# Delta-rule stage of an eight-stage network kernel: pieces in a list-scheduled order, shared PSUM banks, the 31-tap filter on ScalarE and GpSimd

## The chip, the cores and the metric

One core of one Trainium2 chip runs the whole program. The metric is device time in microseconds (us) of one execution. TensorE is called PE, VectorE DVE, ScalarE ACT, GpSimd POOL; DMAs of this stage are issued by the sync engine, SP.

## The reference

Eight stages work one after the other on a residual of 4 batches x 1024 tokens x 128 features in float32: attention, mixture of experts, Mamba block, mixture of experts, sparse attention, a ternary feed-forward block, the delta-rule block, and a ternary feed-forward block. The change lies in the seventh, whose core is this (H = 4 heads, DK = DV = CH = 32, L tokens):

```python
q = _l2norm(q); k = _l2norm(k)
v = v * beta[..., None]; kb = k * beta[..., None]
A = -jnp.einsum('bhncd,bhnsd->bhncs', kb, k) * jnp.tril(ones, -1)
for i in range(1, CH):
    A = A.at[..., i, :].add(jnp.einsum('bhns,bhnsc->bhnc', A[..., i, :], A))
inv = A + eye;  u = inv @ v;  w = inv @ kb
def step(S, xs):
    attn = (qi @ ki.T) * mt
    ui = ui0 - wi @ S
    oi = qi @ S + attn @ ui
    return S + ki.T @ ui, oi
```

Ahead of it q, k and v are projected, convolved causally over 4 tokens and passed through SiLU; beta is a sigmoid of a projection. Beside it v goes through four causal filters (FIR) of 3, 7, 15 and 31 taps for each channel. The four results, v itself and the delta rule's output are the six branches. A gate computes six weights for each head and token, from the hidden state and from each branch's mean absolute value: a GELU layer, a layer to logits, a softmax with a temperature and a floor of 0.05. The weighted sum of the branches is normalised for each head by its root mean square, projected and added to the residual.

## The kernel before, in words

`delta_stage` (L3060) holds features in partitions and tokens in columns: `xT` is 128 x 4096. A batch has 1024 tokens, that is 8 tiles of 128, 32 chunks of 32, 4 pairs of tiles, 2 halves of 512. The work is cut into named pieces, and `schedule()` yields one list of them. Each engine's program walks this one list and emits its own part of every piece, in the list's order. So each engine's queue is in order and fixed, and semaphores alone hold the queues together.

The list is made of: `preparation(b)`, with `raw` (projections of q, k, v), `beta`, `conv` (on DVE: L3595 and L3600), `silu` (ACT, with the squares), `unit` (a product with a block of ones sums the squares over the 32 rows of a head and leaves each sum in all of them, L3258; ACT takes the root, L3486; DVE inverts 128x1024, L3606) and `scale` (POOL L3227 and L3230, DVE L3611 and L3613); `pair_of_tiles(b, pair)`, with `cross` (transposes L3282 and products L3293), four rounds of `level` and `grow` that invert the triangular block (L3266), `uw`, and `keep` (L3341 to L3347), which makes each chunk's transition; and `finish(b)`, with 31 `step`s of the state (PE L3361, DVE L3669), 56 filter taps on DVE (`tap`, L3683 and L3686, one 128x1024 instruction each, one tap between two steps), and then for each half, one after the other: `ruled`, `stat` (ACT takes absolute values, L3524, PE averages them over heads, L3381), `hidden`, `logits`, `mix`, four `token` pieces (six transposes L3413, six products L3727, one reduction L3735), `square`, `root`, `o_scale`, `turn`, `out` (L3754).

What sets the order: `interleave` (L3047) runs the pairs of batch b two ways at a time and puts in, at fixed rates, the preparation of batch b+1 (`AHEAD_RATE` 0.5) and the finish of batch b-1 (`END_RATE` 1.9). The preparation of batch 0 stands alone at the beginning, behind the layer norm of all four batches (`norm.vector`, `norm.scalar`, `norm.tensor`, L275 transposes) and the tempering of the gates (L3569 to L3578), and the finish of batch 3 stands alone at the end.

PSUM has eight banks: the `cross` and `keep` pieces share four (0 to 3), `level`, `grow` and `uw` take turns on banks 4 and 5, and all other pieces take turns on banks 6 and 7 (`wide`, a ring of two). A piece's matmuls wait until the earlier user of their bank has been read.

## Time and profile before

| what | value |
|---|---|
| median of 3 runs | 4448.43 us (4441.52 to 4453.62) |
| the profiled execution, its own time | 4447.42 us |
| its span | 4445.6 us |
| the delta stage in it | 3208.0 to 4188.4 us |
| PE busy over the span | 3357.0 us (76%) |
| DVE busy | 3073.2 us (69%) |
| ACT busy | 2142.4 us (48%) |
| POOL busy | 841.6 us (19%) |
| granted PE clock, mean | 0.826 of full |

The profile is one execution, taken by the hardware profiler. Busy time of an engine is the time in which at least one of its instructions runs. The granted clock is the share of PE's full clock that the throttle let through, 1.0 being 2.4 GHz and 0.5 1.2 GHz. A group of instructions is given as: line, engine, operation, output<-inputs, shapes, count | busy us, mean ns of one | idle us of the engine just ahead of them, and what ended that. Timeline rows begin with the start and the length in us, and end in brackets with idle time ahead of them.

### The profile page before, as it was taken

The page shows a single profiled execution, that of the slowest core. Times are in us where ns is not written, and L with a number is a line of the kernel's source. Part 1 is how long each engine was busy: PE and PEld are TensorE (multiplying, and loading weights), DVE is VectorE, ACT ScalarE, POOL GpSimd, SP SyncE. Part 2 cuts the span into 40 slices and gives each one's busy share as a digit, 9 for nine tenths or more (in the row PEclk, how much of TensorE's full clock was granted, in tenths as well). Part 3 has the DMA queues.
Part 4 walks back from the last instruction along what each step waited for, and adds up shares of the span by engine and source line. Part 5 has one row for each costly group of instructions (what it writes and reads, how often), then busy time and mean ns, then how long its engine had stood idle before and what let it go on. Part 6 is the DMA issues. An engine that isn't in the chain of part 4 may idle for free. (4 is left out here: it accounts for less than half of the span.)

```text
span 4445.6 us, 85630 instructions
## 1 busy us (share of the span) xinstructions
PE 3357.0 (76%) x35482; PEld 1538.8 (35%) x35552; DVE 3073.2 (69%) x4612; ACT 2142.4 (48%) x3613; POOL 841.6 (19%) x734
## 2 busy tenths in 40 slices
PE   6999998996556566699788888879846474653699
PEld 1222222663112111256433333324424353542344
DVE  8889895876787787787634677744455858668543
ACT  4888887664533342266432666656431121110464
POOL 1000100552343344445431000010000000000100
PEclk7999999998667565699899999979966665665799
DMA  3100101000110101000143022010000000000000
GB/s 90 25 22 18 25 8 33 1 2 9 29 26 3 29 0 29 12 18 2 32 74 43 10 39 38 23 49 1 12 2 4 2 3 2 3 3 2 27 1 20
DMA packets 138474, 85.31 MB, mean 19 GB/s; under 512 B 94755, under 2 KB 109749, under 8 KB 137957
## 3 DMA queue, kind: packets, MB, share of 16 engines
q1 hardware_dynamic: 135336, 75.56, 8.0%
q0 software_dynamic: 2688, 4.20, 0.6%
q8 instruction: 283, 4.64, 0.4%
q14 instruction: 103, 0.84, 0.1%
q10 hardware_dynamic: 64, 0.07, 0.0%
HBM read 47.81 MB, written 18.60 MB: 15 GB/s over the span
## 5 line engine op out<-in xcount | busy, mean ns | idle before, releaser
L833 DVE TENSOR_REDUCE attn_peak_halves<-attn_ps 128x2 f32<-128x1024 f32 x512 | 601.6, 1219 | 58.3 <-PE attn_ps L664 50.6
L786 ACT ACTIVATE attn_weights<-attn_ps 128x512 f32<-128x512 f32 x1024 | 531.2, 601 | 100.9 <-PE attn_ps L692 100.8
L1342 PE MATMUL mamba_ps<-mamba_stack,mamba_spread 96*128 96x512 bf16 x512 | 205.1, 519 | 284.9 <-DVE mamba_driven L1566 141.6
L1508 POOL TENSOR_TENSOR mamba_out_c<-mamba_states,mamba_c_rep 128x1024 f32<-128x1024 f32 x128 | 321.8, 2514 | 487.9 <-DVE mamba_states L1572 476.1
L2690 DVE TENSOR_REDUCE sparse_peak<-sparse_ps 128x4 f32<-128x1024 f32 x256 | 309.4, 1224 | 134.1 <-PE sparse_ps L2320 132.6
L142 PE MATMUL moe_ps<-moe_xT_halves,moe_w_halves 128*128 128x512 f16 x1536 | 363.8, 384 | 10.1 <-DVE moe_w_halves L1106 5.9
L1089 POOL TENSOR_TENSOR moe_hidden<-moe_exact,moe_hidden 128x512 f16<-128x512 f32 x256 | 297.0, 1164 | 342.2 <-ACT moe_hidden L1073 333.7
L2550 ACT ACTIVATE sparse_weights<-sparse_ps 128x512 f32<-128x512 f32 (+1 forms) x512 | 272.1, 585 | 176.9 <-PE sparse_ps L2387 89.3
L692 PE MATMUL attn_ps<-attn_q_stack,attn_k_stack 50*128 50x512 f16 x1024 | 321.4, 386 | 30.5 <-ACT attn_weights L786 7.1
L142 PE MATMUL ffn_ps<-ffn_layers,ffn_h_halves 128*128 128x512 f16 x1536 | 334.4, 379 | 3.6 <-ACT ffn_gate L2919 3.6
L1572 DVE TENSOR_TENSOR_SCAN mamba_states<-mamba_ps,mamba_driven 128x1024 f32<-128x1024 f32 x128 | 293.2, 2291 | 33.0 <-ACT mamba_ps L1484 17.3
L1484 ACT ACTIVATE mamba_ps<-mamba_ps,mamba_rates 128x1024 f32<-128x1024 f32 x128 | 138.3, 1086 | 296.5 <-PE mamba_ps L1342 295.9
L664 PE MATMUL attn_ps<-attn_k_stack,attn_q_stack 48*128 48x512 f16 x1024 | 270.7, 395 | 13.9 <-DVE attn_peak_halves L833 12.6
L2991 DVE TENSOR_TENSOR ffn_layers<-ffn_exact,ffn_layers 128x512 f16<-128x512 f32 x192 | 133.1, 695 | 208.1 <-ACT ffn_layers L2908 207.5
L3686 DVE SCALAR_TENSOR_TENSOR delta_branch<-delta_v,delta_fir_w,delta_branch 128x1024 f32<-128x1024 f32 x208 | 271.9, 1307 | 2.5
L704 PE MATMUL attn_ps<-attn_weights,attn_values 128*9 128x512 f32 x2048 | 269.4, 598 | 0.0
L1152 DVE SCALAR_TENSOR_TENSOR moe_exact<-moe_ps,moe_gate 128x512 f32<-128x512 f32 x256 | 175.1, 686 | 84.9 <-ACT moe_gate L1065 79.4
L1566 DVE TENSOR_TENSOR mamba_driven<-mamba_ps,mamba_b_rep 128x1024 f32<-128x1024 f32 x128 | 155.0, 1211 | 94.4 <-PE mamba_ps L1342 94.4
L1065 ACT ACTIVATE moe_gate<-moe_ps 128x512 f32<-128x512 f32 x256 | 152.0, 594 | 137.9 <-PE moe_ps L142 134.0
L142 PEld LDWEIGHTS ffn_ps<-ffn_layers,ffn_h_halves 128*128 128x128 f16 x1536 | 150.0, 98 | 184.3 <-issue 4.5
L692 PEld LDWEIGHTS attn_ps<-attn_q_stack,attn_k_stack 50*128 50x128 f16 x1024 | 80.4, 94 | 374.7 <-ACT attn_weights L786 283.0
L142 PE MATMUL moe_ps<-moe_w_halves,moe_hidden 128*128 128x128 f16 x3072 | 193.6, 220 | 18.3 <-POOL moe_hidden L1089 13.7
(463 smaller groups left out, 6130.1 us busy)
## 6 DMA issues: line engine op xcount, KB each, us to landing
mamba_stack<-mamba_parts SPq DMA_DIRECT2D x96, 128.0 KB, 2.4
sparse_factor<-sp_factor SPq DMA_DIRECT2D x24, 256.0 KB, 3.6
sp_halves<-sparse_parts SPq DMA_DIRECT2D x8, 512.0 KB, 3.0
ffn_h<-in_h SPq DMA_DIRECT2D x4, 1024.0 KB, 7.8
attn_q_stack<-attn_halves SPq DMA_DIRECT2D x96, 32.0 KB
attn_k_stack<-attn_halves SPq DMA_DIRECT2D x96, 32.0 KB
attn_halves<-attn_hp SPq DMA_DIRECT2D x8, 384.0 KB, 3.3
attn_q_stack<-attn_peak_rows SPq DMA_DIRECT2D x128, 2.0 KB
```

What stands on the lines that cost most here:

```text
L142: made = pe.matmul(out, a, b, start=first and i == 0, stop=last and i == 2)
L664: made = pe.matmul(use.slot[:, p, :], q_stack[rows, slot, couple, t * P:(t + 1) * P], k_stack[rows, slot, couple, half_of(keys)], start=Tr ...
L692: pe.matmul(use.slot, k_stack[rows, slot, couple, k * P:(k + 1) * P], q_stack[rows, slot, couple, half_of(half)], start=True, stop=True).t ...
L704: made = pe.matmul(out_acc[32 * h:32 * h + HD + 1, :], values[:, b % 2, k, first + h, :], weights[:, step_no(g, half, k) % 2, h, :], start ...
L786: act.activation(weights[:, at % 2, h, :], use.slot, ACT.Exp).then_inc(*key_act.one())
L833: dve.tensor_reduce(peak_halves[:, turn % PEAKS, keys, at:at + 2], use.slot, AX_X, ALU.max).then_inc(*score_dve.one())
L1089: pool.tensor_tensor(low, exact_sb[:, i % 3, :], hidden[:, i // EB % 3, i % EB, 0, :], ALU.subtract).then_inc(*hidden_low.one())
L1508: pool.tensor_tensor(out_c[:, n % 6, :], states[:, n % 3, :], c_rep[:, b % 2, :], ALU.mult).then_inc(*product_made.one())
L1572: dve.tensor_tensor_scan(states[:, n % 3, :], use.slot, driven[:, n % 2, :], 0.0, ALU.mult, ALU.add).then_inc(*steps_dve.one())
L2550: act.activation(weights[:, at % 2, h, begin:], use.slot[:, begin:], ACT.Exp).then_inc(*key_act.one())
L2690: dve.tensor_reduce(peak[:, at % PEAKS, unit // 2, 4 * r:4 * r + 4], use.slot.rearrange("p h (a k) -> p (h a) k", a=2), AX_X, ALU.max).the ...
L3686: dve.scalar_tensor_tensor(branch[:, n, :], shifted_v, weight, branch[:, n, :], ALU.mult, ALU.add).then_inc(*tapped.one())
```

## The change

One function, `delta_chains()`, names all pieces as chains with their dependences, and a list scheduler, `in_order()`, puts them into one order. It takes assumed costs (`PIECE_COST`), a hop of 0.08 us between engines, and 6 banks; at each turn it takes the piece that could begin first, less 0.02 of its distance to the end. Both ends change with it: the norm's parts are pieces of their own, batch by batch (`moments`, `norm_root`, `apply`, `features`), and the tempering comes after the first `scale`; `ruled`, `stat` and `token` are chains of their own, the statistics one piece for each branch, with `ruled` needing only the steps of its half.

PSUM: banks 0, 1, 2, 3, 6, 7 are shared; `cross` and `keep` still take 0 to 3 together, `level` and `grow` of one way keep one bank (4 or 5), `uw` takes shared banks, the statistics hold bank 6 or 7 from their first piece to their last.

Lengths: the squares are summed with tokens in partitions (`sums`), root and inverse are taken on 128x64, and `spread` multiplies with the identity to bring each inverse back to the 32 rows of its head, from where ACT copies it to `lengths`.

The 31-tap filter is a chain `long_tap`: for each tap and half ACT writes v times its weight into `weighted`, and POOL adds it onto the branch, which lies in `q_all`. ACT writes a half again only when POOL has added the tap before. DVE keeps 25 taps a batch.

The token sum has two products of 128x384 in place of six of 128x128, and three additions in place of the reduction. The weights' loads are reordered, with a semaphore of their own for the first four.

```diff
+LONG = len(FIR_TAPS) - 1
-TAP_ORDER = [(k, n) for k in range(max(FIR_TAPS)) for n, count in enumerate(FIR_TAPS) if k < count]
+TAP_ORDER = [(k, n) for k in range(max(FIR_TAPS)) for n, count in enumerate(FIR_TAPS) if n != LONG and k < count]
+STAT_ORDER = [4, 0, 1, 2, 3, 5]
+PIECE_COST = {
...
+    "level": [("pe", 0.8), ("dve", 0.45)], "grow": [("pe", 1.05), ("dve", 0.9)],
+    "uw": [("pe", 1.2), ("act", 0.8)], "keep": [("pe", 2.5), ("dve", 0.85), ("act", 0.45)],
+    "step": [("pe", 0.35), ("dve", 0.22)], "tap": [("dve", 1.25)], "long_tap": [("act", 1.35), ("pool", 2.6)],
...
+HOP, URGENCY = 0.08, 0.02
+SHARED = [0, 1, 2, 3, 6, 7]
...
+def delta_chains():
...
+        if b:
+            needs["raw", b, 0] += [("scale", b - 1)]
...
+        if b >= 2:
+            needs["beta", b] += keeps(b - 2)
+        if b >= 3:
+            needs["conv", b, 1] += [("token", b - 3, 1, TPC - 1)]
...
+        needs["ruled", b, half] += [("step", b, CPB // 2 - 2 if half == 0 else CPB - 2)]
...
+        needs["stat", b, half, 1] += [("tap", b, len(TAP_ORDER) - 1)]
+        needs["stat", b, half, 4] += [("long_tap", b, FIR_TAPS[LONG] - 1)]
+        needs["stat", b, half, 5] += [("ruled", b, half)]
...
+def in_order():
...
+            begin, _ = run(piece, ready, Counter(free), filled)
+            score = begin - URGENCY * to_end[piece]
+            if best is None or score < best[0]:
+                best = (score, which, piece, ready, filled)
...
@@ gpsimd
+                def long_tap(b, k):
+                    for half in range(HALVES if k else 0):
+                        so_far = long_of(b)[:, columns(half)]
+                        pool.wait_ge(*long_scaled.at(HALVES * (b * FIR_TAPS[LONG] + k) + half + 1))
+                        if k > 1:
+                            pool.wait_ge(*long_added.at(added_by(b, k - 1, half)))
+                        pool.tensor_tensor(so_far, so_far, weighted[:, half, :], ALU.add).then_inc(*long_added.one())
@@ tensor
-                norm.tensor(pe)
-                pe.wait_ge(*loads.at(16 * len(given)))
-                pe.wait_ge(*begun.at(1))
-                pe.wait_ge(*gained.at(1))
-                pe.wait_ge(*norm.featured.at(CHUNKS))
...
+                def sum_squares(b):
...
+                    for n in (1, 0):
+                        for t in range(TPB):
+                            at = (n * TPB + t) * KH
+                            made = pe.matmul(use.slot[:, at:at + KH], lengths[:, n, t * P:(t + 1) * P], first_of_head,
+                                             start=True, stop=True)
...
+                def spread_over_heads(b, n):
...
+                        for t in range(TPC):
+                            for h in range(KH):
+                                of_head = roots[:, 1, n, half * TPC + t, h:h + 1].broadcast_to([P, KD])
+                                made = pe.matmul(use.slot[KD * h:KD * (h + 1), t * P:(t + 1) * P], of_head,
+                                                 net.ident[:], start=True, stop=True)
...
@@ scalar
+                def long_tap(b, k):
...
+                    for half in range(HALVES):
+                        if k > 1:
+                            act.wait_ge(*long_added.at(added_by(b, k - 1, half)))
...
+                        act.activation(weighted[:, half, :] if k else long_of(b)[:, columns(half)],
+                                       v_all[:, b % 3, at:at + BANK], ACT.Copy,
+                                       scale=fir_w[:, tap:tap + 1]).then_inc(*long_scaled.one())
@@ vector
-                def invert_lengths(b, n):
-                    dve.wait_ge(*wide_act.at(one("unit", b, n).over))
-                    dve.reciprocal(lengths[:, n, :], lengths[:, n, :]).then_inc(*unit.one())
+                def invert_lengths(b):
+                    dve.wait_ge(*wide_act.at(one("sums", b).over))
+                    dve.reciprocal(roots[:, 1].rearrange("p n t h -> p (n t h)"),
+                                   roots[:, 0].rearrange("p n t h -> p (n t h)")).then_inc(*unit.one())
...
+                        dve.tensor_tensor(by_head(product[:, some, :]),
+                                          by_head(use.slot[:, 0:3 * P].rearrange("p (n d) -> p n d", n=3)),
+                                          weight.broadcast_to([P, 3, KH, KD]), ALU.mult).then_inc(*wide_dve.one())
...
+                    settle(dve.tensor_tensor(product[:, 0:3, :], product[:, 0:3, :], product[:, 3:6, :], ALU.add))
+                    settle(dve.tensor_tensor(product[:, 0, :], product[:, 0, :], product[:, 1, :], ALU.add))
...
-                    dve.tensor_reduce(o[:, t, :], product[:].rearrange("p n d -> p d n"), AX_X,
-                                      ALU.add).then_inc(*combined.one())
+                    dve.tensor_tensor(o[:, t, :], product[:, 0, :], product[:, 2, :], ALU.add).then_inc(*combined.one())
```

## Rows read from the trace of the kernel before

**Rows 1.** Busy time over stretches of the delta stage; its opening, middle, taps, end, whole
```profile
core 0: us, PE busy (x) PEld busy (x) DVE busy (x) ACT busy (x) POOL busy (x), PEclk, DMA share, GB/s
3208.00:3287.50 79.50, 25.02 (x58) 11.84 (x59) 49.60 (x126) 26.37 (x39) 4.30 (x2) 0.61 0.06 16
3287.50:4038.00 750.50, 443.74 (x15472) 325.26 (x15470) 504.28 (x843) 154.70 (x299) 16.64 (x6) 0.65 0.01 3
4038.00:4111.20 73.20, 12.17 (x376) 7.91 (x376) 71.04 (x88) 0.59 (x1) 0.00 (x0) 0.50 0.00 1
4111.20:4188.40 77.20, 47.65 (x288) 29.84 (x288) 31.73 (x84) 22.79 (x32) 0.00 (x0) 0.65 0.00 1
3208.00:4188.40 980.40, 528.59 (x16192) 374.85 (x16192) 656.65 (x1139) 204.45 (x371) 20.94 (x8) 0.63 0.01 4
```

**Rows 2.** Groups of DVE instructions of the stage, shapes kept apart
```profile
L3686 DVE SCALAR_TENSOR_TENSOR delta_branch<-delta_v,delta_fir_w,delta_branch 128x1024 f32<-128x1024 f32 x208 | 271.9, 1307 | 2.5
...
L3606 DVE RECIPROCAL delta_raw<-delta_raw 128x1024 f32<-128x1024 f32 x8 | 52.1, 6537 | 19.2 <-ACT delta_raw L3486 19.2
...
L3735 DVE TENSOR_REDUCE delta_o<-delta_product 128x128 f32<-128x768 f32 x32 | 46.8, 1461 | 1.1
...
L3727 DVE TENSOR_TENSOR delta_product<-delta_ps,delta_logits 128x128 f32<-128x128 f32 x192 | 40.8, 282 | 0.7
...
L3634 DVE TENSOR_TENSOR delta_t<-delta_ps,delta_masks 128x256 f32<-128x256 f32 x64 | 26.8, 421 | 62.6 <-PE delta_ps L3266 62.1
...
L3754 DVE TENSOR_TENSOR residual<-residual,delta_ps 128x512 f32<-128x512 f32 x8 | 5.5, 688 | 21.5 <-PE delta_ps L3430 21.5
```

**Rows 3.** The stage's waits, one row
```profile
ACT delta_absolute L3524 <- DVE delta_branch L3692: 174.3, 8, 73.1
```

**Rows 4.** Timelines of POOL and DVE around the scaling, batches 0 and 2
```profile
3280.50 2.00 POOL L3227 TENSOR_TENSOR delta_qk<-delta_qk,delta_raw 128x1024 f32<-128x1024 f32 x1 [275.57 <-DVE delta_raw L3606]
...
3282.53 3.34 DVE L3611 TENSOR_TENSOR delta_kbq<-delta_qk,delta_beta 128x1024 f32<-128x1024 f32 x1 [2.11 <-POOL delta_qk L3227]
...
3502.91 2.88 POOL L3227 TENSOR_TENSOR delta_qk<-delta_qk,delta_raw 128x1024 f32<-128x1024 f32 x1 [153.39 <-DVE delta_raw L3606]
...
3504.51 5.65 DVE L3686 SCALAR_TENSOR_TENSOR delta_branch<-delta_v,delta_fir_w,delta_branch 128x1024 f32<-128x1024 f32 x2
```

**Rows 5.** Earlier stages: a POOL product (MoE), a DVE product by min/median/max (Mamba)
```profile
L1089 POOL TENSOR_TENSOR moe_hidden<-moe_exact,moe_hidden 128x512 f16<-128x512 f32 x256 | 297.0, 1164 | 342.2 <-ACT moe_hidden L1073 333.7
...
L1551 DVE TENSOR_TENSOR mamba_temp<-mamba_temp,mamba_x x8: 1225/3250/3251, 1129.5 to 1699.1; 128x1024 f32<-128x1024 f32 x8
```

**Rows 6.** Groups of ACT instructions of the delta stage
```profile
L3524 ACT ACTIVATE delta_absolute<-delta_branch 128x512 f32<-128x512 f32 x40 | 24.4, 628 | 190.8 <-DVE delta_branch L3692 174.3 <-PE delta_ps L3381 16.5
...
L3534 ACT ACT_TABLE_LOAD x8 | 10.3, 1283 | 0.1
```

**Rows 7.** PE groups of the stage; the last row gives durations min/median/max
```profile
L3258 PE MATMUL delta_ps<-delta_raw,delta_block_ones 128*128 128x512 f32 x32 | 22.0, 825 | 22.3 <-ACT delta_raw L3480 22.3
...
L3402 PE MATMUL delta_ps<-delta_w_logit,delta_hidden 128*128 128x24 f32 x128 | 22.5, 297 | 6.2 <-ACT delta_hidden L3534 6.2
...
L3266 PE MATMUL delta_ps<-delta_n,delta_at 32*32 32x32 f32 x4096 | 63.7, 223 | 35.6 <-issue 13.2 <-DVE delta_n L3629 12.5 <-DVE delta_n L3644 9.7
...
L3244 PE MATMUL delta_ps<-delta_xT,delta_w_qkv x48: 592/1061/1222, 3233.0 to 3655.7; 128*128 128x512 f32 x48
```

**Rows 8.** Timeline of PE in the stage's opening
```profile
3214.46 2.14 PE L275 MATMUL delta_ps<-w_ident,delta_branch 128*128 128x128 f32 x8 [7.20 <-DVE delta_branch L215]
...
3233.02 7.17 PE L3244 MATMUL delta_ps<-delta_xT,delta_w_qkv 128*128 128x512 f32 x9 [4.87 <-DVE delta_eps L3578]
...
3262.98 5.68 PE L3258 MATMUL delta_ps<-delta_raw,delta_block_ones 128*128 128x512 f32 x8 [19.62 <-ACT delta_raw L3480]
```

**Rows 9.** Timeline of DVE: two steps of the state in the last batch
```profile
4040.25 0.18 DVE L3669 TENSOR_TENSOR delta_state<-delta_ps,delta_keep 128x32 f32<-128x32 f32 x1
...
4041.01 0.18 DVE L3669 TENSOR_TENSOR delta_state<-delta_ps,delta_keep 128x32 f32<-128x32 f32 x1
```

**Rows 10.** Timeline of PE: the statistics of a half in the last batch
```profile
4112.71 7.44 PE L3381 MATMUL delta_ps<-delta_absolute,delta_stat_select 128*128 128x512 f32 x12 [33.67 <-ACT delta_absolute L3524]
```

More of the change, by code:

```diff
@@ L1 @@
-from collections import Counter
+from collections import Counter, defaultdict
 from contextlib import ExitStack
@@ new lines, with __init__, take @@
+class Banks:
+    def __init__(self):
+        self.n, self.over, self.before = Counter(), Counter(), {}
+    def take(self, kind, by, slot, *filled):
+        self.n[kind] += 1
+        self.over[kind, by] += 1
+        earlier = {self.before[bank] for bank in filled if bank in self.before}
+        newest = {key: max(count for other, count in earlier if other == key) for key, _ in earlier}
+        for bank in filled:
+            self.before[bank] = ((kind, by), self.over[kind, by])
+        return Use(slot, self.n[kind], sorted(newest.items()), self.over[kind, by])
@@ L3154, in finish @@
-        def finish(b):
-            taps = [("tap", b, i) for i in range(len(TAP_ORDER))]
-            work = [[("step", b, c), taps[c]] for c in range(CPB - 1)] + [[tap] for tap in taps[CPB - 1:]]
-            for half in range(HALVES):
-                work += [[(what, b, half)] for what in ("ruled", "stat", "hidden", "logits", "mix")]
-                work += [[("token", b, half, t)] for t in range(TPC)]
-                work += [[(what, b, half)] for what in ("square", "root", "o_scale", "turn", "out")]
-            return work
@@ L3186, in delta_stage @@
-        uses, crosses, turns = {}, {}, {}
-        for piece in schedule():
-            if piece[0] in takes:
-                ring, by, count = takes[piece[0]]
-                uses[piece] = [ring.take(by) for _ in range(count)]
+        order, taken = in_order()
+        psum, uses, crosses, turns, kept = Banks(), {}, {}, {}, {}
+        by_act = ("features", "raw", "beta", "sums", "spread", "heads", "uw", "hidden", "turn")
+        all_heads = lambda width: ps[:, 0:CPT, 0:width * KC].rearrange("p a (m t n) -> p a m t n", m=2, t=2)
@@ new lines, in delta_stage @@
+        for piece in order:
+            if piece[0] in BANKS_OF:
+                by = "act" if piece[0] in by_act else "dve"
+                uses[piece] = [psum.take("wide", by, ps[:, bank, :], bank) for bank in taken[piece]]
+            if piece[0] == "stat" and piece[3] == 0:
+                uses[piece] = [psum.take("stat", "act", ps[:, bank, :], bank) for bank in taken[piece]]
+            if piece[0] in ("level", "grow"):
+                bank = 4 + piece[2] % 2
+                uses[piece] = [psum.take("diag", "dve", ps[:, bank, 0:8 * KC], bank)]
@@ L3196, in delta_stage @@
         pair_no = lambda b, pair: b * PAIRS + pair
+        last_keep = lambda b: max((("keep", b, pair) for pair in range(PAIRS)), key=lambda piece: kept[piece])
         grid_of = lambda slot: slot.rearrange("p (h t n) -> p h t n", h=KH, t=2)
@@ L3220, in _ @@
+                for piece in order:
+                    if piece[0] == "long_tap":
+                        long_tap(*piece[1:])
                     if piece[0] == "scale":
                         b = piece[1]
-                        qk, kbq = qk_all[:, b % 2], kbq_all[:, b % 2]
-                        pool.wait_ge(*unit.at(2 * b + 2))
+                        q, k, kbq = q_all[:, b % 3, :], k_all[:, b % 2, :], kbq_all[:, b % 2]
+                        pool.wait_ge(*wide_act.at(one("spread", b, 0).over))
```

542 lines of the change are left out of this document (333 added, 209 removed).

## The prediction, made blind

> **What bounds the kernel now.** I read first the busy times over the stretches of the delta stage [rows 1]. The stage takes 980.4 us (3208.0 to 4188.4), and no other stage is touched. In it the vector engine (DVE) is busy 656.7 us, TensorE (PE) 528.6, ScalarE (ACT) 204.5, GpSimd (POOL) 20.9: no engine fills the stage, and what counts is how badly they overlap. The stretches tell three different stories. The opening of 79.5 us is one chain through the first batch. The middle of 750.5 us has PE at 59% and DVE at 67%. The last 150.4 us are nearly serial: 73.2 us in which DVE alone works (71.0 busy, PE 12.2), then 77.2 us of gating, token sums and output projection for two halves, one after the other. Second, the groups of DVE work [rows 2]: the filter taps (L3686) are 271.9 us, 41% of DVE; the two full-width reciprocals a batch (L3606) 52.1; the weighted sum over branches (L3727, L3735) 87.6. Third, one line of the waits [rows 3]: ACT stands 174.3 us ahead of the absolute values, 73.1 of them once, because the queue puts the whole block of taps ahead of `ruled`. So the stage is bound by the written order at both ends and by DVE, in bursts, between them.
>
> **Against which time.** The profiled execution took 4447.4 us by its own time, 4445.6 of it span, 1.0 us under the median of 4448.4. I work against 4447.4; the 1.0 us is below what matters. Some 0.3% (13 us) is what a measurement of this kernel can tell from no change.
>
> **DVE.** (a) The 31-tap branch leaves it: 30 instructions a batch of L3686's form, 120 x 1.307 = 156.8 us, and four opening multiplies that cost no more than such a tap each, 160 in all [rows 2]. (b) Eight reciprocals of 1024 columns (52.1) become four of 64 columns; scaled by columns one is 0.4 us, so 50 goes. (c) A group of 128 tokens now costs (40.8 + 46.8)/32 = 2.74 us. After: two products of 384 columns, between the 421 ns of 256 columns and the 688 of 512 [rows 2], so 0.55 each; one addition of 384 columns, 0.55; two of 128, 0.28 each: 2.2 us. Over 32 groups 17 us goes. DVE is left with 656.7 - 160 - 50 - 17 = 430 us.
>
> **POOL.** It gains 30 additions x 2 halves x 4 batches = 240 of 128x512. Bounds: half of the 2.00 us that an undisturbed addition-sized operation of 1024 columns takes [rows 4], 1.00 us, and the 1164 ns of the MoE stage's 512-column product [rows 5]. I take 1.10: 264 us, with the 17 that stays (undisturbed) 281.
> DVE and POOL don't run such work side by side. At 3282.53 a DVE product that is 1.2 us by itself took 3.34: it waited for POOL's to end. From 3502.91 the two take turns: POOL's 2.00 becomes 2.88 behind one tap, and two taps take 5.65 us around POOL's operations [rows 4]. In the Mamba stage the same product takes 1.225 us or 3.251 [rows 5]. So every overlap of a two-SBUF-input operation is paid by one side. Of DVE's remainder such work is 88 taps and 36 convolution taps of the same form at 1.2 [rows 2] and some 70 us of small ones, about 220 us; in a middle of 600 us it stands in POOL's way a third of the time. 240 x 1/3 x 0.6 us is about 50 us for POOL, and DVE, by the same count the other way, loses about 65 us. At none this is 0 (the operations never meet), at most 264 us (DVE waits out every addition).
> The Trainium skill (SBUF — State Buffer, Who interferes with whom) says that the pair of ports is an exclusive lock for the whole instruction, and that a reduction never contends while a two-input addition does. The trace agrees on the lock; by the second clause the 96 new additions of the token sum are exposed where the 32 reductions were not, which would give back up to half of the 17 us of (c).
> The Trainium skill (GPSIMD Engine Reference, 3.1 Elementwise) keeps elementwise work on DVE, since GpSimd takes 1.96 times as long, 4497 ns for 2048 columns. An estimate by that page is 1.12 us an addition, 270 us in all; the rule would bite only if POOL's chain were the longest, which is the rival B below.
>
> **ACT.** 248 scaled copies of 128x512 from SBUF, at the 628 ns of the absolute values [rows 6]: 156 us. Roots over 64 columns in place of 16 of 512 save 8, plain copies of the spread lengths give them back. Interleaving may split runs of one table: 10 loads more at 1283 ns [rows 6] would be 13. ACT comes to 360 to 375 us of about 730: not a bound by itself, but its queue is in order, and a long tap waits there for POOL's addition one tap before.
>
> **PE.** Out: the block-ones product, 22.0 us [rows 7]. In: per batch 32 small instructions for the sums, at 0.15 us like the logits' twelve in about 1.0 us or up to 0.3 (their mean each), so 5 to 10, I take 6; and 128 instructions that spread an inverse over 32 rows. If four head rows overlap as the 32x32 blocks do (4096 instructions in 63.7 us busy [rows 7]) these are 5 to 6 us a batch; if not at all, at 0.2 us, 26. I take 6, because the trace's narrow tiles do overlap: 48 us in for 22 out. PE is left with 528.6 + 26 = 555 us, with an end of 635. It is now the busiest engine, and the cover for every other edit.
>
> **The opening.** Before, the first projection starts at 3233.0 after all four batches' norms and the gates' tempering; the first batch's transposes start at 3214.5 and take 2.1 us [rows 8]. Only they are wanted: with 0.6 us of eviction [rows 6] the projection starts at about 3217.5, 15.5 earlier. Then 30 us unchanged to the squares. From there to POOL's scaling it was 17.5 us [rows 4, 8]; now 6 (sums) + 1.6 (table, root) + 0.5 + 6 (spread) + 1.2 = 15.3. The opening goes from 79.5 to about 62 us (bounds 58 to 90). The loads' reordering costs nothing: four early weights are issued by about 3210, long before they are read; the norms of batches 1 to 3 slip under convolution waits.
>
> **The end.** After the last `keep` of batch 3: 15 steps at no more than 0.76 us, the beat that they keep with a short tap between them [rows 9], 11; `ruled` 2.6; of the 77.2/2 = 38.6 us a half takes, the 7.4 us of six statistics [rows 10] are done beforehand save the last (1.2), so 32 [rows 1]; of the second half, whose statistics and gates run under the first's tokens, some 20 remain. That is 66, taken as 70, against 150.4 plus the few us of keeps before it. The long taps of batch 3 must be ready: at 2 x (1.10 + 0.2) + 0.1 = 2.7 us a tap they take 84 us a batch and start at its scaling, some 150 us before the last keep, so about 60 us are to spare.
>
> **The middle.** PE has 555 - 25 (opening) - 45 (end) = 485 us to do; DVE 430 - 35 - 30 = 365 and 65 of waiting, 430; POOL some 270 + 50. Steps, taps and both ways of a batch are separate chains, and six banks replace a ring of two, so PE is rarely without work; but order is fixed from assumed costs and every queue waits in it, and the four banks of a cross or keep must all be empty. The middle of before had PE at 59%. I take 81%: 596 us.
>
> **Sum.** 62 + 596 + 70 = 728 us for 980.4: 252 less, 4447.4 - 252 = 4195 us.
>
> **Rivals.** *B, the shared ports decide.* POOL is slowed by taps, ACT stands at the long taps behind it, and PE's evictions behind ACT. For it: [rows 4, 5]. Against: most of DVE's small work reads PSUM, and 60 us are to spare. Price at full exclusion: 430 + 281 in series + 240 handovers x 0.1, with 65 us at the ends where neither works: 800; 4267 us.
> *C, PE packs better and its clock rises.* The granted clock was 0.65 over the middle at 59% busy and 0.50, the lower of the two levels (1.2 of 2.4 GHz), where PE was nearly idle [rows 1]; a wide projection takes 592 ns at best and 1222 at worst [rows 7]. With a denser queue some 300 us of wide instructions would fall by a quarter. 555 - 75 = 480, 410 of it in the middle, at 80% 510 us: stage 640, 4107 us. The Trainium skill (TensorE: Matmul & The Clock Gate, Part 1) says that activity releases the throttle, which speaks for C.
> *D, slower than before.* The long taps run in lockstep: ACT copies a half, POOL waits for a DVE tap, adds, and only then ACT goes on. A half then costs ACT 0.63 + 1.2 + 1.1 = 2.93 us: 248 x 2.93 = 727, plus ACT's other 180, 62 at the start and 55 at the end: 1024, 4491 us. It decides from 2.75 us a half. Against: there are two half buffers, and the copy of one goes under the addition of the other.
> *E, the order doesn't do what it says.* Real durations differ, the fixed queues drift, and the middle stays near 70% PE: 690 us, stage 822, 4289 us. I count it with B.
>
> **How the numbers follow.** My case 0.53, B and E 0.23, C 0.20, D 0.04. The range 4100 to 4300 holds my case with its bounds (opening to 90, PE to 635 at 81%: +110; no port waits: -40), C, B and E; beyond it lie D and some 0.1 of the tails of C and E. Faster by over 0.3%: all but D and a little of E, 0.95; within 0.3% 0.01; slower 0.04.
>
> **What would show it.** Right: the stage near 730 us; L3686's form down to 88 instructions; POOL with 240 additions of 1.0 to 2.3 us, mean near 1.3; taps on DVE partly stretched to 2.3 us; the first projection near 3217; no stretch with DVE alone at the end; PE above 75% of the middle. Wrong: ACT idle ahead of the scaled copies for over 100 us, waiting for POOL (B, D); PE under 70% with waits on `keep`, or on evictions (E); the clock above 0.8 (C); spreading above 15 us a batch.

## The result, and the profile after

The changed kernel takes 4396.66 us (median of four runs, 4390.06 to 4402.06), the kernel before on the same chip 4445.43: a ratio of 0.9887 with a 95% interval of 0.9864 to 0.991. That is 49 us less where 252 were forecast. The profiled execution is the one of 4390.06 us. In it the delta stage, from the first batch statistics on the vector engine to the last addition to the residual, goes from 979.7 to 924.1 us. Below, "stage" is always this stretch of a kernel's own profile.

Busy time over the stretches that answer to [rows 1]: the opening up to the first cross product, the middle up to the last `keep`, the end, and the whole.
```profile
core 0: us, PE busy (x) PEld busy (x) DVE busy (x) ACT busy (x) POOL busy (x), PEclk, DMA share, GB/s
3206.00:3261.00 55.00, 28.12 (x198) 19.55 (x198) 27.96 (x87) 22.38 (x32) 4.31 (x2) 0.69 0.09 24
3261.00:4038.30 777.30, 456.39 (x15928) 344.25 (x15928) 487.64 (x746) 314.57 (x556) 375.21 (x246) 0.65 0.01 3
4038.30:4130.40 92.10, 55.67 (x674) 34.76 (x674) 49.70 (x115) 24.69 (x35) 0.00 (x0) 0.70 0.00 1
...
3206.00:4130.40 924.40, 540.18 (x16800) 398.56 (x16800) 565.30 (x946) 361.64 (x622) 379.52 (x248) 0.66 0.02 4
```
Both ends are shorter than before: 55 us for 79.5 (62 were forecast), and 92 for 150.4 (70 were forecast). The middle is not: it is longer than before (777.3 against 750.5), and TensorE is still at 59% of it (456.4 / 777.3), the share it had before. Here the forecast said 596 us at 81%. Of the 196 us of stage that are missing (924.4 against 728), the middle has 181 and the end 22, and the opening gives 7 back.

The groups of instructions of the stage, shapes kept apart, for what the change added or touched [rows 2, 6]:
```profile
L3359 POOL TENSOR_TENSOR delta_q<-delta_q,delta_weighted 128x512 f32<-128x512 f32 x240 | 361.1, 1534 | 357.5 <-ACT delta_weighted L3734 357.5
L3734 ACT ACTIVATE delta_weighted<-delta_v,delta_fir_w 128x512 f32<-128x512 f32 x240 | 166.8, 722 | 82.7 <-POOL delta_q L3359 82.5
L3898 DVE SCALAR_TENSOR_TENSOR delta_branch<-delta_v,delta_fir_w,delta_branch 128x1024 f32<-128x1024 f32 x88 | 146.7, 1667 | 0.8
...
L3950 DVE TENSOR_TENSOR delta_product<-delta_product 128x384 f32<-128x384 f32 x32 | 26.6, 831 | 1.1
L3951 DVE TENSOR_TENSOR delta_product<-delta_product 128x128 f32<-128x128 f32 x32 | 26.5, 828 | 1.1
...
L3413 PE MATMUL delta_ps<-delta_block_ones,delta_raw 128*128 128x4 f32 x128 | 23.6, 321 | 2.6 <-ACT delta_raw L3660 2.6
...
L3424 PE MATMUL delta_ps<-w_ident,delta_roots 128*32 128x128 f32 x512 | 20.9, 331 | 0.4 <-issue 0.3
L3955 DVE TENSOR_TENSOR delta_o<-delta_product 128x128 f32<-128x128 f32 x32 | 20.8, 648 | 1.1
L3808 DVE SCALAR_TENSOR_TENSOR delta_v<-delta_raw,delta_conv_w,delta_v 128x1024 f32<-128x1024 f32 x12 | 20.3, 1695 | 0.0
```
The 88 taps are there, but each takes 1667 ns where it took 1307; the two additions of 128 columns take 828 and 648 ns where 0.28 us was forecast, and the sums and the spreading on TensorE take 44.5 us in all, where 48 were forecast.

The waits of TensorE in the stage (what it waited for: us in total, times, longest):
```profile
PE delta_ps L3534 <- DVE delta_state L3878: 107.5, 81, 9.8
PE delta_ps L3433 <- issue: 58.8, 40, 2.2
PE delta_ps L3466 <- DVE delta_kat L3833: 31.9, 5, 8.8
PE delta_ps L3433 <- DVE delta_n L3838: 28.8, 10, 7.1
PE delta_ps L3556 <- ACT delta_absolute L3710: 23.2, 19, 3.6
PE delta_ps L275 <- DVE delta_branch L196: 22.9, 2, 16.0
```
Two rows stand out. Ahead of the steps of the state TensorE waits 107.5 us for DVE. And 58.8 us, 40 times, it "waits" in the small blocks of the level products (L3433) for nothing that the profile shows. Before, this row had less than half of that:
```profile
PE delta_ps L3266 <- issue: 22.1, 19, 2.1
```
The timeline of TensorE in one such stretch (start, length, what it ran, in brackets the idle time ahead of it):
```profile
3303.57 1.20 PE L3433 MATMUL delta_ps<-delta_n,delta_at 32*32 32x32 f32 x69 [1.29 <-issue]
3304.54 1.04 PE L3433 MATMUL delta_ps<-delta_t,delta_n 32*32 32x32 f32 x58
3307.30 1.21 PE L3433 MATMUL delta_ps<-delta_t,delta_n 32*32 32x32 f32 x70 [1.72 <-issue]
3308.63 1.00 PE L3433 MATMUL delta_ps<-delta_n,delta_at 32*32 32x32 f32 x57
3311.03 1.20 PE L3433 MATMUL delta_ps<-delta_n,delta_at 32*32 32x32 f32 x71 [1.40 <-issue]
```
From halt to halt there are 69 + 58 = 127 and 70 + 57 = 127 matmuls, each with a weight load, and 3.7 us. The halts fall in the midst of a piece, where the code waits for nothing. Of the 40, 39 last 0.8 to 2.2 us and one 0.3. The DMA table of the stage has a queue that fits this count:
```profile
q8 instruction: 133, 2.18, 1.0%
```
133 packets and 2.18 MB are 16.4 KB a packet, and 33,600 matmuls and weight loads over 133 packets are 253 a packet: about one packet for each 127 matmuls with their loads.

The trace has the time of each packet too, and it says more than the count. Over all lines of the stage, 69 pauses of TensorE are put down to "issue" (96.5 us in all). Of these, 67 end 1.2 to 1.6 us after the queue's last packet before them is through; of the 174 other pauses of TensorE 7 do. From one such pause to the next there are 127 matmuls or a multiple of it, to within two, 59 times in 68. So these pauses are waits for the packets of this queue, and what the packets bring is TensorE's instructions. Where TensorE works less densely most packets come without a pause: there are 133 packets and 69 pauses.

So there were three suspects for the missing 196 us of stage: the shared access of DVE and GpSimd, the order itself with its round trips between TensorE and DVE, and the supply of TensorE's instructions.

### The profile page after: what moved, and what is told of

Same layout as the page of the kernel before. It is cut to its first block and busy times, and to the rows that moved or that the text cites. A ratio compares the mean times of both kernels' runs of the same rounds, so it can differ in the third digit from the quotient of the medians.

```text
span 4388.3 us, 87460 instructions
## 1 busy us (share of the span) xinstructions
PE 3362.3 (77%) x36090; PEld 1558.9 (36%) x36160; DVE 2982.4 (68%) x4420; ACT 2298.6 (52%) x3864; POOL 1198.0 (27%) x974
## 5 line engine op out<-in xcount | busy, mean ns | idle before, releaser
L3359 POOL TENSOR_TENSOR delta_q<-delta_q,delta_weighted 128x512 f32<-128x512 f32 x240 | 361.1, 1534 | 357.5 <-ACT delta_weighted L3734 357.5
L3734 ACT ACTIVATE delta_weighted<-delta_v,delta_fir_w 128x512 f32<-128x512 f32 x240 | 166.8, 722 | 82.7 <-POOL delta_q L3359 82.5
```

Of the source, the lines that this page charges most:

```text
L3359: pool.tensor_tensor(so_far, so_far, weighted[:, half, :], ALU.add).then_inc(*long_added.one())
```

## Experiments, first batch: what the long filter costs

All start from the changed kernel unless another is named. The kernel before took 4461.18 us on this chip. Chips differ by more than some of these edits do, so the stages are compared with each other. Most experiments are single executions, and the batches ran on different chips. The one kernel that was profiled twice, on two chips, gave stages of 766.3 and 770.4 us, so a difference of some 5 us or less is not to be read.

**GpSimd's additions on 8 columns** (the long filter's sum is left out but for these columns).
```
-  pool.tensor_tensor(so_far, so_far, weighted[:, half, :], ALU.add)
+  pool.tensor_tensor(so_far[:, 0:8], so_far[:, 0:8], weighted[:, half, 0:8], ALU.add)
```


> POOL's 240 additions of the long filter work on 8 columns in place of 512, so most of the 31-tap sum is left out; order, waits and ACT's copies stay. The delta stage of the changed kernel takes 924 us. Ports theory (what DVE and POOL take from each other, some 120 us of stretched DVE work, ate the gain): the stage falls by 120 us or more, to 800 or less. Order theory (PE and DVE wait for each other in one fixed order, the stretching is only part): it falls by 30 to 70, to 855 to 895. ACT theory (ACT's queue stands at the long taps): it falls by over 80 as well, and the next run by more.

Measured: 4311.26 us, stage 846.2, 78 less. Groups of its DVE instructions:
```profile
L3898 DVE SCALAR_TENSOR_TENSOR delta_branch<-delta_v,delta_fir_w,delta_branch 128x1024 f32<-128x1024 f32 x88 | 112.9, 1283 | 0.9
...
L3950 DVE TENSOR_TENSOR delta_product<-delta_product 128x384 f32<-128x384 f32 x32 | 17.9, 558 | 1.1
L3808 DVE SCALAR_TENSOR_TENSOR delta_v<-delta_raw,delta_conv_w,delta_v 128x1024 f32<-128x1024 f32 x12 | 15.3, 1278 | 0.0
...
L3955 DVE TENSOR_TENSOR delta_o<-delta_product 128x128 f32<-128x128 f32 x32 | 9.4, 293 | 1.1
L3951 DVE TENSOR_TENSOR delta_product<-delta_product 128x128 f32<-128x128 f32 x32 | 9.3, 292 | 1.1
```
The same instructions fall from 1667 to 1283 ns (taps), from 1695 to 1278 (convolution), and from 831, 828 and 648 to 558, 292 and 293 (token additions). The timelines of the changed kernel show one such meeting: while GpSimd adds without a break, a token addition of 128x128 takes 1.24 us, about as long as one of GpSimd's own, and 0.29 right after GpSimd's last.
```profile
3512.26 16.14 POOL L3359 TENSOR_TENSOR delta_q<-delta_q,delta_weighted 128x512 f32<-128x512 f32 x12 [2.71 <-ACT delta_weighted L3734]
```
```profile
3513.98 1.24 DVE L3951 TENSOR_TENSOR delta_product<-delta_product 128x128 f32<-128x128 f32 x1
...
3528.85 0.29 DVE L3951 TENSOR_TENSOR delta_product<-delta_product 128x128 f32<-128x128 f32 x1
```
DVE's busy time goes from 565.3 to 446.7: GpSimd costs DVE 119 us, of which 34 are in the taps, 17 in the convolutions and 37 in the token additions. The stage falls by 78. That is the price of GpSimd's additions as a whole and not of the shared access alone: the edit also takes 277 us of work off GpSimd (379.5 to 102.4) and shortens ScalarE's waits for it (82.5 to 4.9). But the stage is still 846 us with no long filter to speak of, so the larger part of what was missing lies elsewhere.

**ScalarE's copies on 8 columns too.**
```
-  act.activation(weighted[:, half, :] if k else long_of(b)[:, columns(half)],
-                 v_all[:, b % 3, at:at + BANK], ACT.Copy,
+  wide = 8 if k else BANK
+  act.activation((weighted[:, half, :] if k else long_of(b)[:, columns(half)])[:, 0:wide],
+                 v_all[:, b % 3, at:at + wide], ACT.Copy,
```


> ACT's 240 scaled copies are on 8 columns too, so the long filter costs neither ACT nor POOL anything; same order. Ports and order theory: within 15 us of the run with narrow additions alone. ACT theory: at least 40 us below it.

Measured: 4293.54 us, stage 831.9, 14 less than with narrow additions, while ACT falls from 351.8 to 255.6 us. ACT's 96 us were nearly all hidden.

**The long taps back on DVE**, the order planned with 1.25 us for each; all else of the change stays.
```
-    "step": [("pe", 0.35), ("dve", 0.22)], "tap": [("dve", 1.25)], "long_tap": [("act", 1.35), ("pool", 2.6)],
+    "step": [("pe", 0.35), ("dve", 0.22)], "tap": [("dve", 1.25)], "long_tap": [("dve", 1.25)],
...
+                def long_tap(b, k):
...
+                        dve.scalar_tensor_tensor(long_of(b), shifted_v, weight, long_of(b), ALU.mult, ALU.add).then_inc(*long_added.one())
```


> The long taps go back to DVE as their own chain of 31 full-width taps, and the same scheduler orders all pieces with 1.25 us for each; banks, ends, lengths and token sum stay as changed. By the loads alone (my prediction's way) DVE gets 160 us more and the stage gets longer by 60 us or more, to over 985. Ports theory: 120 us of stretching go, 160 of work come: 940 to 980. Order theory: the engines have room and no lock, 860 to 925: moving the filter was worth nothing.

Measured: 4414.65 us, stage 945.4. So the move of the filter brought 21 us, and everything else (order, banks, ends, lengths, token sum) 34 (979.7 to 945.4).

**The token's three additions as one reduction again.**
```
-  settle(dve.tensor_tensor(product[:, 0:3, :], product[:, 0:3, :], product[:, 3:6, :], ALU.add))
-  settle(dve.tensor_tensor(product[:, 0, :], product[:, 0, :], product[:, 1, :], ALU.add))
...
-  dve.tensor_tensor(o[:, t, :], product[:, 0, :], product[:, 2, :], ALU.add).then_inc(*combined.one())
+  dve.tensor_reduce(o[:, t, :], product[:].rearrange("p n d -> p d n"), AX_X, ALU.add).then_inc(*combined.one())
```


> The three additions of a token sum are one reduction over six again; all else as changed. Additions took 831, 828 and 648 ns where they were forecast at 550, 280 and 280. Ports theory: 73.9 us of additions become 46.8 of reductions that never wait, and POOL gets through sooner: the stage falls by 20 to 40. Order theory: by 0 to 15.

Measured: 4386.63 us, stage 919.0, DVE 538.0 us for 565.3.
```profile
L3953 DVE TENSOR_REDUCE delta_o<-delta_product 128x128 f32<-128x768 f32 x32 | 47.8, 1494 | 1.1
```
The reduction is the cheaper one here: the additions add to 831 + 828 + 648 = 2307 ns beside GpSimd's work, against 558 + 292 + 293 = 1143 beside its narrow additions, and the reduction takes 1494, hardly more than before (1461). DVE's 27 us give 5 at the end, which is within what two executions differ by: an engine that has time to spare.

## Second batch: order, round trips, instruction supply

**Another order of the same pieces.** The planner's table starts from the durations that the profile shows, scaled kind by kind (`keep` is 5.17 for 4.5 measured, `temper` 13.55 for 5.0), and an offset for each kind is added to its score. The values were found by a search off the chip; what they are worth is what the chip shows. Only the order differs, and with it the shared bank that a piece takes; the instructions and what they compute are the same.
```
-    "uw": [("pe", 1.2), ("act", 0.8)], "keep": [("pe", 2.5), ("dve", 0.85), ("act", 0.45)],
...
+    "uw": [("pe", 2.01), ("act", 1.17)], "keep": [("pe", 5.17), ("dve", 0.92), ("act", 0.69)],
...
+LATER = {"o_scale": -0.95, "cross": -1.16, "root": -14.5, "ruled": 0.85, "mix": -1.14, "moments": 0.8, "conv": 0.64, "norm_root": -24.59,
...
-HOP, URGENCY = 0.08, 0.02
+HOP, URGENCY = 0.05, 0.0145
...
-            score = begin - URGENCY * to_end[piece]
+            score = begin - URGENCY * to_end[piece] + LATER.get(piece[0], 0.0)
```


> Same instructions as the changed kernel; only the order of the pieces is another, planned from the durations that the trace of the changed kernel shows (keep on TensorE 4.5 us where the planner had 2.5, first convolution 5.2 for 4.2, token 3.3 for 1.95, and so on), with an offset for each kind of piece. The stage is 924 us long in the changed kernel. If the order is what holds the stage (waits between engines that another order could fill): 20 to 90 us less, stage 835 to 905, with TensorE's busy time unchanged near 540 and its share of the stage up from 58% to 60 to 65%. If the shared access of VectorE and GpSimd sets the stage whatever the order: within 15 us of 924, and the busy time of both unchanged (565 and 380). If the order on record is already near what the round trips allow: the same or slower.

Measured: 4276.49 us against 4442.77 for the kernel before, stage 809.9: 114 us less, more than the highest figure expected. The same 100 us by the clock (one of the stretches in which the two differ most), first with the order on record, then with the new one, and below that the new one's whole stage:
```profile
3406.00:3506.00 100.00, 52.06 (x1265) 33.55 (x1269) 73.23 (x90) 42.17 (x68) 55.16 (x30) 0.63 0.01 2
```
```profile
3406.00:3506.00 100.00, 70.76 (x2008) 49.74 (x2007) 72.35 (x114) 48.73 (x81) 47.18 (x32) 0.69 0.01 3
3206.50:4016.40 809.90, 530.68 (x16800) 397.75 (x16800) 549.76 (x943) 362.24 (x621) 384.05 (x248) 0.67 0.02 4
```
The order on record leaves stretches in which TensorE has little to do beside the steps: 1265 matmuls here, 52% busy. In the new order the small blocks of the next batch lie between them: 2008 matmuls, 71%. Over the stage the engines are as busy as before to within 16 us each. Of the 114 us, 105 are idle time of TensorE, which goes from 924.1 - 540.2 = 384 to 279 us.

**Long taps on DVE with an order of their own**: the kernel with all taps on DVE, and an edit of the same kind of its table, offsets and two constants, with values that were searched for this arrangement.


> The third experiment (long filter back on VectorE, GpSimd with nothing but the scales; stage 945 us) with its order planned from the durations measured there. If the move of the filter matters little and the order much: stage 840 to 900, so faster than the changed kernel at 924 without any help from GpSimd. If VectorE's load (594 us) is what holds this arrangement: 930 to 950, no gain from a better order. TensorE's busy time stays near 545 and VectorE's near 590 either way.

Measured: 4238.57 us, stage 766.3, well under the 840 to 900 expected. The order is worth 179 us to this arrangement (945.4 to 766.3), and it now beats the one with GpSimd and ScalarE by 44 (766.3 against 809.9). TensorE is at 68% (521.8), DVE at 77% (591.2). Each has its own order, so the 44 us compare the best found of each, not the filter's place alone.

**No recurrence between chunks** (left out: each step's product reads the batch's first state, and TensorE does not wait for the previous step).
```
-                    else:
-                        pe.wait_ge(*wide_dve.at(one("step", b, c - 1).over))
...
-                                         state[rows, b % 2, c, :], start=True, stop=True)
+                                         state[rows, b % 2, 0, :], start=True, stop=True)
```


> Left out: the recurrence from one chunk's state to the next; each step's product reads the batch's first state, so TensorE does not wait for VectorE's previous step. All instructions and the order stay. In the changed kernel TensorE stands 107 us ahead of the steps, waiting for VectorE. If these round trips hold the stage: 60 to 110 us less (stage 815 to 865). If another wait stands right behind them (VectorE with its additions held up by GpSimd must still do each piece in order): 0 to 35 us less, and the idle time moves to the waits ahead of the levels, the crosses and the free banks. If the instruction supply is the wait there, nothing changes.

Measured: 4386.0 us, stage 918.1, 6 less. Waits of TensorE in it:
```profile
PE delta_ps L3554 <- ACT delta_absolute L3708: 38.9, 21, 6.8
...
PE delta_ps L3532 <- DVE delta_state L3876: 30.3, 18, 3.9
...
PE delta_ps L3466 <- DVE delta_state L3876: 24.5, 3, 8.4
```
The largest row of the waits, 107.5 us, was worth 6 at most. The wait fell to 30.3, and the idle time moved to the pieces behind: to the statistics (38.9 for 23.2) and to the crosses, which now wait for the steps' banks (24.5).

**Fewer, wider matmuls in the level products** (left out: the heads' own left factors; all four take the first head's).
```
-                        for h in range(KH):
-                            for c in range(CPT):
...
-                                made = pe.matmul(grid[rows, h, tile, :], left[rows, h, tile, :],
-                                                 right[rows, h, tile, :], start=True, stop=True)
+                        for c in range(CPT):
...
+                            made = pe.matmul(grid[rows, :, tile, :], left[rows, 0, tile, :],
+                                             right[rows, :, tile, :], start=True, stop=True)
```


> Left out: in the products of the five levels, the four heads' own left factors (all heads take the first head's); a product of 4 heads is one matmul of 128 columns instead of 4 of 32, so 8 matmuls for 32 in 160 pieces, 3840 fewer and as many weight loads fewer, of about 34,000 instructions of TensorE in the stage. Columns streamed are the same. If TensorE halts because its instructions come in batches (a stop of 1.2 to 2.6 us at every 127 matmuls, one 16 KB packet of the instruction queue each): the packets of the stage fall from 133 to about 103, the idle time inside pieces from 98 us to 65 to 80, TensorE's busy time by 40 to 90, and the stage by 25 to 80. If these halts have another cause (data, banks): packets fall but the idle time inside pieces stays near 98, and the stage falls by under 25.

Measured: 4312.45 us, stage 835.7, 88 less. The count of the expectation was off: the pieces are 128 and each product is two recorded matmuls, so 6144 matmuls and as many loads go, 12,288 instructions. At 256 a packet that is 48 packets, and the table has exactly 48 fewer:
```profile
q8 instruction: 85, 1.39, 0.7%
```
The level products' groups show that the halts in them are gone ("issue" no longer stands among the releasers; over matmuls and loads of this line it fell from 125.5 us, 89 times, to 2.1, 8 times):
```profile
L3432 PE MATMUL delta_ps<-delta_n,delta_at 32*32 32x128 f32 x1024 | 53.2, 342 | 42.1 <-DVE delta_n L3837 29.0 <-DVE delta_n L3852 11.6
...
L3432 PE MATMUL delta_ps<-delta_t,delta_n 32*32 32x128 f32 x768 | 39.4, 343 | 9.8 <-DVE delta_t L3842 8.9
```
TensorE's busy time falls 38 us (540.2 to 502.2) and its idle time 50 (384.2 to 333.7); over the whole stage the pauses put down to "issue" fall from 96.5 us, 69 times, to 37.8, 27 times. So fewer instructions are worth 88 us here, but the runs don't part the shorter busy time from the halts.

## Third batch: which part of the order, and what is left

**Measured durations alone**, without scaling and offsets.
```
-    "uw": [("pe", 1.2), ("act", 0.8)], "keep": [("pe", 2.5), ("dve", 0.85), ("act", 0.45)],
...
+    "uw": [("pe", 1.9), ("act", 1.1)], "keep": [("pe", 4.5), ("dve", 0.8), ("act", 0.6)],
```


> The changed kernel with one edit: the planner's table of durations holds those measured in its trace; its rule (earliest start, less 0.02 of the way to the end) stays and there are no offsets. The stage is 924 us with the table on record and 810 us with the same table of measured durations, scaled, plus offsets for each kind of piece. If the wrong durations of the table were what spoilt the order: 810 to 860. If the greedy rule itself is the fault, whatever its durations: 890 to 940, within 35 us of the stage on record.

Measured: 4362.08 us, stage 892.7. So right durations give 31 us of the 114, and 83 come from the scaling, the offsets and the two constants together. It is the figure that was expected if the rule of the earliest start is at fault and not its table. But the better order has another table too, and which of its edits does it was not tried, so that stays open.

**The new order with narrow additions** (the same part left out as in the first experiment).


> The replanned order (stage 810) with GpSimd's additions of the long filter on 8 columns instead of 512 (the filter is left out but for them). With the order on record this took 78 us off the stage (924 to 846). If the shared access costs the same whatever the order: 725 to 745. If a better order hides VectorE's stretched instructions: 780 to 800. Between them, 745 to 780: part is hidden.

Measured: 4215.64 us, stage 744.7, 65 less than the new order alone (78 in the order on record). A better order hides only a sixth of the price of GpSimd's additions. Together the order and these additions account for 924.1 - 744.7 = 179 of the 196 us that were missing.

**Fewer matmuls, taps on DVE, new order** (the same left factors left out).


> The kernel with all taps on VectorE and the first replanned order (stage 766) with the heads' own left factors left out of the level products: 8 matmuls of 128 columns in place of 32 of 32 in 160 pieces, as in the fourth experiment of the batch before, which took the stage from 924 to 836 and the packets of TensorE's instructions from 133 to 85. If the supply of instructions holds this arrangement too: 60 to 90 us less, 676 to 706. If VectorE, busy 591 of 766 us, takes over: 10 to 45 us less, 720 to 756.

Measured: 4217.12 us, stage 743.8, 23 less than with the same order (766.3), for 88 in the order on record:
```profile
3212.40:3956.30 743.90, 510.40 (x10656) 352.83 (x10656) 587.33 (x1067) 202.44 (x375) 21.34 (x8) 0.71 0.01 4
```
DVE is busy 587 of 744 us, 79%, as expected for the case that it takes over. What fewer instructions are worth depends on what lies beside them.

**A second search of the order, timed.**


> All taps on VectorE, order planned with the measured durations and a second set of offsets (further searched). The first such order gave a stage of 766 us and 4238.6 for the whole. If the order still holds the stage: 745 to 765, whole 4217 to 4238. If the arrangement is at what its instructions allow: 765 to 780, whole 4237 to 4252. Against the kernel before the ratio should be 0.948 to 0.957.

Measured: 4246.7 us median against 4453.09 for the kernel before, ratio 0.9538 (0.9517 to 0.956), stage 778.0: no better than the first.

## Fourth batch: the best version, timed

**All taps on DVE, first new order.**


> The kernel with all taps on VectorE and the first replanned order, as in the second batch, now timed. One run gave 4238.6 us. If that was typical: ratio to the kernel before 0.950 to 0.956, so about 3.5 to 4% under the changed kernel too. If the single run was a lucky one: near the second replanned order, 0.954 or above.

Measured: 4232.98 us (4227.62 to 4235.71, four runs) against 4445.92 for the kernel before: ratio 0.9517 (0.9495 to 0.9538). Its stage:
```profile
3204.70:3975.20 770.50, 527.41 (x16800) 390.11 (x16800) 591.20 (x1067) 202.71 (x375) 21.84 (x8) 0.71 0.02 5
```
That is 4.8% under the kernel before and, by the two ratios (0.9517 / 0.9887), 3.7% under the changed one, without ScalarE or GpSimd in the filter. It computes the same as both.

**The same with the reduction.**


> All taps on VectorE with the first replanned order (stage 766), and the token's sum as the one reduction of the kernel before (1.46 us) in place of three additions (0.56 + 0.29 + 0.29 undisturbed, so 1.14): VectorE has 32 times 0.32 = 10 us more. If VectorE (591 of 766 us) is near the bound: 3 to 10 us more than the run without this edit. If the order holds the stage: within 3 us of it.

Measured: 4238.49 us, ratio 0.9532 (0.9512 to 0.9553), stage 771.1 against 770.4; DVE 601 us for 591. Beside hardly any GpSimd work the additions are the cheaper form for DVE. All four executions with the reduction are longer (4236.37 to 4239.58 us) than all four with the additions (4227.62 to 4235.71), by 5.5 us in the median, which is 0.13%. The profiled stages differ by 0.7 us only, so whether these 5.5 us lie in the stage is not shown.

**The new order without the recurrence** (same part left out as above).


> The changed kernel with the replanned order (stage 810) and without the recurrence between chunks (each product reads the batch's first state). With the order on record this took 6 us off, though TensorE stood 107 us there; in the replanned order it stands 83 us there. If round trips between TensorE and VectorE are still covered by another wait right behind them: 0 to 20 us less. If the better order has left the steps as the last wait: 40 to 80 us less, stage 730 to 770.

Measured: 4273.48 us, stage 807.4 against 809.9. The step's round trips are covered in either order.

## Why the prediction was wrong

- **The sign and the opening: right; the end: half.** The first projection starts 7.5 us into the stage where 9.1 were forecast, and the opening is 55 us for 62. The end is 92 for 70, a term sized 22 us too small: in it TensorE still waits 18.1 us ahead of the steps and ACT 16.5 us for the last taps.
- **The engines' own work: near.** TensorE 540 us for 555, ACT 362 in 360 to 375, the spreading 5.2 us a batch for 6. DVE undisturbed is 447 us in the run with narrow additions, for 430.
- **"The middle of before had PE at 59%. I take 81%: 596 us." This step failed.** It stayed at 59%, and the middle took 777 us. Nor did any run get there: the forecast needed TensorE busy 76% of the stage (555 of 728), and the highest share measured is 69% (515.6 of 744.7, with the new order and narrow additions). The step rested on separate chains and six banks giving TensorE always something to do; the sentence beside it, that the order is fixed from assumed costs and every queue waits in it, was the true one. The same instructions in another order take 114 us off (with the taps on DVE 179). Rival E, "real durations differ", was the nearest of the four, at too small a chance and too mild a price (70%). Its sign came in part: TensorE is under 70%, but its largest wait is ahead of the steps (107.5 us) and not of the `keep`s (10.5). Its reason was in part right: true durations alone are worth 31 of the 114 us, and which of the planner's other edits brought the rest was not tried.
- **"DVE, by the same count the other way, loses about 65 us."** A term mis-sized. DVE loses 119 us, GpSimd is busy 379.5 us where 281 and about 50 of waiting were forecast, and the stage loses 78 (65 in the better order). Two things were off. The addition is 1.26 us undisturbed (the shortest of 240), not 1.10, and 1.53 on average. On 8 columns the shortest takes 0.19 us and the median 0.20, so a scaling by columns alone leaves out a fixed part. Worked out from the two shortest, it is an estimate of 2.1 ns a column and 0.18 us besides, which for 2048 columns would be 4.50 us. (The Trainium skill, GPSIMD Engine Reference, 3.1 Elementwise, has 4497 ns for 2048 columns, and the trace agrees with that figure; what the trace does not bear out is the 1.12 us that was scaled down from it.) And the meetings were counted by time shares of large operations; the short additions of the token sum, counted as "small ones", lost most in proportion (292 to 828 ns). In the end the move of the filter was worth 21 us in the order on record, and less than nothing between the best orders found for each. Rival B's sign, ScalarE idle for over 100 us ahead of the scaled copies, did not come: it was 82.5.
- **The Trainium skill's lock between the two engines (SBUF — State Buffer, Who interferes with whom)** holds in both clauses. The token additions stretch and the reduction doesn't (1494 ns in the fourth experiment, 1461 before; DVE falls by 27 us with it). By that clause the prediction had up to half of the token sum's 17 us given back; in fact all of it was, and more: 831 + 828 + 648 ns in place of one 1461.
- **Missed altogether: the supply of TensorE's instructions.** [rows 7] already had the row "issue 13.2" in the level products. The prediction used the row for its busy time alone. Fewer instructions win back 88 us in the order on record and 23 where DVE is the fuller engine; in both, shorter busy time (38 and 11 us) is part of that.
- **Rival C, the clock: wrong.** The granted clock is 0.66 over the stage for 0.63, between its two levels; even at 68% busy it is 0.71.
- **A sum of the range.** The upper bounds of its own case were put at +110. They are 28 us of opening and (635 - 555) / 0.81 = 99 of TensorE, 127 in all, so 4322 us and not inside the 4300 of the range. The result lies beyond either.
- The parts overlap. The order and GpSimd's additions together account for 179 of the 196 us; with the stage of 744.7 us the forecast's 728 is nearly there, but only with the filter's additions left out.

## What to carry to other kernels

A list-scheduled order is worth what its rule and its durations are worth: measure the pieces in the trace, plan again, and time more than one order before the order is blamed or praised, since the same instructions gave stages from 810 to 924 us, and measured durations alone gave 893. Price a row of waits by taking the wait away: the largest one, 107.5 us, was worth 6 at most. And work moved to GpSimd was paid for here by VectorE's instructions with two inputs in SBUF beside it, the short ones most.

## What the runs showed of the hardware

- In dense runs of 32x32 products TensorE halts 0.8 to 2.2 us after 127 matmuls with their weight loads, about every 3.7 us. The instruction queue moves one 16 KB packet for each 253 to 256 instructions, and 67 of 69 such halts of the stage end 1.2 to 1.6 us after a packet is through.
- Beside GpSimd's additions of 128x512 a DVE addition of 128x128 takes 828 ns on average, beside its additions of 128x8 292. A reduction of 768 columns in the same place costs DVE less than the three additions that replace it.
- GpSimd adds 128x512 in 1.26 us at best and 1.53 on average beside DVE's work, and 128x8 in 0.19 us at best, 0.20 in the median and 0.36 on average.
